# A two-layer transformer kernel: loads of the front in other pieces and order, weight folds at other places, fewer zero products

## What is computed

```python
    def _L0_xattn_ref(modality1, modality2, ln1_g, ln1_b, ln2_g, ln2_b, Wq, bq, Wk, bk, Wv, bv, Wo, bo):
...
        x1 = layernorm(modality1, ln1_g, ln1_b)
        x2 = layernorm(modality2, ln2_g, ln2_b)
        q = x1 @ Wq + bq
        k = x2 @ Wk + bk
        v = x2 @ Wv + bv
        scores = jnp.einsum('bqe,bke->bqk', q, k) * scaling
        attn = jax.nn.softmax(scores, axis=-1)
        ctx = jnp.einsum('bqk,bke->bqe', attn, v)
        return ctx @ Wo + bo
...
            h = jax.nn.gelu(ctx @ w1.T + b1, approximate=False)
            route_logits = (h @ w2.T + b2) / (jnp.abs(tau) + 0.1)
...
            gx = gi @ gru_wih.T + gru_bih
            gh = hs @ gru_whh.T + gru_bhh
...
            slot_values = S_new @ wv.T + bv
            out = jnp.einsum('bts,bsd->btd', alpha, slot_values)
            return out @ wo.T + bo
...
    x = x + _L0_xattn_ref(_layernorm(x, axis=-1), ctx_768, ...)
    x = x + _L0_ffn_ref(_layernorm(x, axis=-1), ...)
    x = x + _L1_xattn_ref(_layernorm(x, axis=-1), ctx_768, ...)
    x = x + _L1_ffn_ref(_layernorm(x, axis=-1), ...)
    return x
```

## Time and profile before

| | |
|---|---|
| median of three runs | 552.25 us (551.52 to 552.89) |
| profiled execution, first to last instruction (span) | 551.06 us |
| profiled execution, time with what lies around the span | not recorded apart; the fastest run is 551.52 us |
| TensorE busy | 538.4 us, 98% |
| VectorE, ScalarE, GpSimd busy | 284.0, 254.1, 168.7 us |
| moved by DMA | 74.30 MB, mean 135 GB/s |

### The profile page before, as it was taken

One profiled execution on the slowest core, in us unless ns is written; L12 is line 12 of the kernel. 1 busy time (PEld: TensorE's weight loads), 2 busy tenths in 40 slices (PEclk: granted clock), 3 DMA queues, 4 the chain that ended last, 5 costly groups with the idle time before them and its releaser, 6 DMA issues.

```text
span 551.1 us, 11061 instructions
## 1 busy us (share of the span) xinstructions
PE 538.4 (98%) x3967; PEld 444.4 (81%) x3968; DVE 284.0 (52%) x847; ACT 254.1 (46%) x587; POOL 168.7 (31%) x152
## 2 busy tenths in 40 slices
PE   9999999999999999999999889999999999999995
PEld 7887878777655676777777679999999999999995
DVE  4867676988562776855788865722212111212110
ACT  1343476263346767687787834542222222222221
POOL 2211000002145222332222043354335454445533
PEclk9999999999999999999999999999999999999999
DMA  8940000000110000300470657968788888898733
GB/s 320 403 141 1 2 0 2 0 1 2 38 39 0 2 2 1 116 1 2 135 287 7 227 172 244 318 187 268 221 246 219 248 229 236 239 255 238 239 66 38
DMA packets 28651, 74.30 MB, mean 135 GB/s; under 512 B 5600, under 2 KB 20320, under 8 KB 23360
## 3 DMA queue, kind: packets, MB, share of 16 engines
q1 hardware_dynamic: 18592, 61.87, 31.9%
q0 software_dynamic: 7488, 10.39, 10.6%
q10 hardware_dynamic: 2528, 1.48, 0.9%
HBM read 62.88 MB, written 10.85 MB: 134 GB/s over the span
## 4 chain that ended last, share of the span: by engine, by line
PE 93%; ACT 4%; DVE 1%; issue 1%; POOL 0%; DVEq 0%; POOLq 0%
PE ps L897 64%; PE ps L1193 12%; PE ps L901 11%; ACT ring L617 2%; PE ps L1041 1%; PE ps L1050 1%; ACT ring L624 1%; PE ps L1053 1%; PE ps L1044 1%; PE ps L981 1%; PE ps L1024 1%; ACT HF L629 0%; ACT ring L658 0%; POOL out_x L422 0%; PE ps L1122 0%
## 5 line engine op out<-in xcount | busy, mean ns | idle before, releaser
L897 PE MATMUL ps<-keep,arena 128*128 128x128 f32 (+2 forms) x976 | 114.9, 274 | 0.0
L897 PEld LDWEIGHTS ps<-keep,arena 128*128 128x128 f32 x976 | 112.8, 192 | 1.5 <-issue 1.1
L2014 DVE TENSOR_TENSOR keep<-keep,ps 128x512 f32<-128x512 f32 x39 | 26.8, 686 | 145.7 <-PE ps L897 124.2
L422 POOL DMA_INDIRECT out_x<-arena,row_no x38 | 59.9, 1576 | 102.1 <-DMA out_x<-arena,row_no 65.2
L1193 PE MATMUL ps<-arena,keep 128*128 x312 | 73.7, 380 | 0.1
L665 ACT COPY keep<-ps 128x256 f32<-128x256 f32 x39 | 14.5, 372 | 107.1 <-PE ps L901 103.8
L381 POOL TENSOR_TENSOR ring<-arena,keep 128x512 f32<-128x512 f32 x32 | 33.5, 1049 | 96.9 <-PE ps L897 79.8
L1193 PEld LDWEIGHTS ps<-arena,keep 128*128 128x128 f32 x312 | 56.4, 190 | 6.6 <-issue 0.3
L617 ACT ACTIVATE ring<-ps,mx 128x128 f32<-128x128 f32 x192 | 52.3, 403 | 6.2 <-DVE mx L1714 6.2
L897 PE MATMUL ps<-ring,arena 128*32 128x128 f32 (+1 forms) x640 | 53.1, 348 | 1.5 <-ACT ring L624 1.4
L373 POOL TENSOR_TENSOR var_x<-var_x,minus_half 128x4 f32<-128x4 f32 x16 | 16.5, 1036 | 115.8 <-DVE var_x L1570 115.8
(11 more groups left out here) (266 smaller groups left out, 816.2 us busy)
## 6 DMA issues: line engine op xcount, KB each, us to landing
arena<-in_w SPq DMA_DIRECT2D x29, 1024.0 KB
w_first<-in_w SPq DMA_DIRECT2D x10, 1024.0 KB
arena<-in_w SPq DMA_DIRECT2D x8, 512.0 KB, 7.3
keep<-in_keep SPq DMA_DIRECT2D x1, 3115.0 KB, 20.8
ring<-in_fold SPq DMA_DIRECT2D x1, 2112.0 KB, 12.7
arena<-in_x SPq DMA_DIRECT2D x4, 512.0 KB, 10.5
arena<-in_ctxT SPq DMA_DIRECT2D x4, 512.0 KB, 7.1
arena<-in_ctx SPq DMA_DIRECT2D x4, 384.0 KB, 11.2
```

Of the source, the lines that this page charges most:

```text
L422: pool.indirect_dma_start(out=out_d, out_offset=bass.IndirectOffsetOnAxis(ap=rows_at, axis=0), in_=YO[t % DEEP], in_offset=None, compute_o ...
L897: ins = pe.matmul(out, w, m, start=(k == 0), stop=(k == len(pairs) - 1))
L2014: dve.tensor_tensor(HA[r % 2], HA[r % 2], ps[:, 2 * (r % 2) + 1, :], ALU.mult).then_inc(act_ok, 1)
```

## The change

The fold weights are packed in another order (whh last), and loaded in four pieces (768, 768, 576 and 768 KB), each with its own semaphore; the rest of `keep` is loaded in two (288 KB of w1 and w2, and the remainder). The first part of `keep` and of the fold weights now stand ahead of the context of group 0. The zero stores move from ScalarE to SyncE, behind the transposed contexts. TensorE has 6 zero products in place of 16 at the start and none in the query bias; fold_value stands directly behind fold_query, and fold_slots ahead of turn_x(1). The bias columns of fold_value go to another bank. ScalarE scales qk and makes two of the four columns of `spread`, ahead of its first copy; VectorE no longer does. On VectorE norm_x(0) stands ahead of norm_c(0), and the folds stand at other places between statistics and norms.

```diff
--- before.py
+++ after.py
@@ -55,12 +55,12 @@
     ("aW1", KD * H1), ("aW2", H1 // P * D), ("gate", KD * 32),
     ("above16", P // 2), ("ones16", P // 2), ("col_no", P), ("before_group", NGRP * NGRP), ("before_expert", NE * NE), ("tile_start", B), ("pick_start", NPICK * B), ("tile_no", NT), ("tile_first", NT), ("expert_no", NE),
 ])
-KEEP_A = KEEP["w1"][0]
+KEEP_A, KEEP_B = KEEP["w1"][0], KEEP["wih"][0]
 FOLD, FOLD_N = columns([
     ("WqT", KD * D), ("WkT", KD * D), ("Wq", KD * D), ("Wo", KD * D), ("WvT", KD * D), ("Wv", KD * D),
-    ("whh", KD * 3 * D), ("fwv", KD * D), ("fwoT", KD * D), ("slots", KD * NSLOT),
+    ("fwv", KD * D), ("fwoT", KD * D), ("slots", KD * NSLOT), ("whh", KD * 3 * D),
 ])
-FOLD_A = FOLD["Wo"][0]
+FOLD_A, FOLD_B, FOLD_C = FOLD["Wo"][0], FOLD["fwv"][0], FOLD["whh"][0]
 ROWS, ROWS_N = columns([
     ("bo", D), ("slot_scale", NSLOT), ("b2", NSLOT), ("tau", 1), ("fbo", D), ("ab2", D),
 ])
@@ -232,7 +232,7 @@
 
 
         keep_in, fold_in, rows_in = sem("keep_in"), sem("fold_in"), sem("rows_in")
-        keep_in2, fold_in2 = sem("keep_in2"), sem("fold_in2")
+        keep_in2, keep_in3, fold_in2, fold_in3, fold_in4 = (sem(t) for t in ("keep_in2", "keep_in3", "fold_in2", "fold_in3", "fold_in4"))
         x_in = [sem(f"x_in{g}") for g in range(NG)]
         c_in = [sem(f"c_in{g}") for g in range(NG)]
         y_in = [sem(f"y_in{g}") for g in range(NG)]
@@ -244,9 +244,9 @@
         names += "".join(f" var_{m} rs_{m}" for m in norms)
         s = {n: sem("s_" + n) for n in names.split()}
         fold_ps, fold_ok = sem("fold_ps"), sem("fold_ok")
-        half_set = sem("half_set")
-
-        blank_set, blank_out, hot_ok, placed = sem("blank_set"), sem("blank_out"), sem("hot_ok"), sem("placed")
+        set_ok = sem("set_ok")
+
+        blank_out, hot_ok, placed = sem("blank_out"), sem("hot_ok"), sem("placed")
         cols_known, cols_far, columns_ok = sem("cols_known"), sem("cols_far"), [sem(f"columns_ok{k}") for k in range(NPICK)]
         counts_read = sem("counts_read")
         pair_ok, pair_ps, pair_known, pair_sum, pair_added = (sem(t) for t in ("pair_ok", "pair_ps", "pair_known", "pair_sum", "pair_added"))
@@ -310,6 +310,8 @@
         def _(sp):
             def rows_of(g):
                 sp.dma_start(X[g], x_g[g]).then_inc(x_in[g], 16)
+
+            def context_rows_of(g):
                 sp.dma_start(CH[g][:, :, 0:DC], c_g[g]).then_inc(c_in[g], 16)
 
             def context_of(g):
@@ -324,17 +326,34 @@
                 if g < EB // GB:
                     sp.dma_start(early_g[g], XH4[g]).then_inc(stored[g], 16)
 
+            def some_keep(lo, hi, landed):
+                sp.dma_start(keep[:, lo:hi], keep_d[:, lo:hi]).then_inc(landed, 16)
+
+            def some_fold(lo, hi, landed):
+                sp.dma_start(ring[:, lo:hi], fold_d[:, lo:hi]).then_inc(landed, 16)
+
             rows_of(0)
-            sp.dma_start(keep[:, 0:KEEP_A], keep_d[:, 0:KEEP_A]).then_inc(keep_in, 16)
-            sp.dma_start(ring[:, 0:FOLD_A], fold_d[:, 0:FOLD_A]).then_inc(fold_in, 16)
+            some_keep(0, KEEP_A, keep_in)
+            some_fold(0, FOLD_A, fold_in)
+            context_rows_of(0)
+            some_fold(FOLD_A, FOLD_B, fold_in2)
             rows_of(1)
-            sp.dma_start(ring[:, FOLD_A:FOLD_N], fold_d[:, FOLD_A:FOLD_N]).then_inc(fold_in2, 16)
+            context_rows_of(1)
+            some_fold(FOLD_B, FOLD_C, fold_in3)
             sp.dma_start(rows[:, :], rows_d.partition_broadcast(P)).then_inc(rows_in, 16)
             rows_of(2)
-            sp.dma_start(keep[:, KEEP_A:KEEP_N], keep_d[:, KEEP_A:KEEP_N]).then_inc(keep_in2, 16)
+            context_rows_of(2)
+            some_keep(KEEP_A, KEEP_B, keep_in2)
+            some_fold(FOLD_C, FOLD_N, fold_in4)
             rows_of(3)
+            context_rows_of(3)
+            some_keep(KEEP_B, KEEP_N, keep_in3)
             for g in range(NG):
                 context_of(g)
+            sp.wait_ge(set_ok, 2)
+            for n in range(2):
+                sp.dma_start(out_d[B * S + n * P:B * S + n * P + P, :], blank[:, 0:D]).then_inc(blank_out, 16)
+            sp.dma_start(xh_d[B * S:B * S + P, :], blank[:, :]).then_inc(blank_out, 16)
             store(0)
             store(1)
             sp.wait_ge(stored[0], 48)
@@ -422,9 +441,9 @@
                 pool.indirect_dma_start(out=out_d, out_offset=bass.IndirectOffsetOnAxis(ap=rows_at, axis=0),
                                         in_=YO[t % DEEP], in_offset=None, compute_op=ALU.add).then_inc(added, 16)
 
-            pool.memset(minus_half[:, :], -0.5).then_inc(half_set, 1)
-            pool.wait_ge(half_set, 1)
-            pool.memset(blank[:, :], 0.0).then_inc(blank_set, 1)
+            pool.memset(minus_half[:, :], -0.5).then_inc(set_ok, 1)
+            pool.wait_ge(set_ok, 1)
+            pool.memset(blank[:, :], 0.0).then_inc(set_ok, 1)
             for g in range(NG):
                 pool.memset(CH[g][:, :, DC:DC + 1], 1.0)
                 pool.memset(CH[g][:, :, DC + 1:D], 0.0).then_inc(s["ch_pad"], 1)
@@ -529,6 +548,15 @@
                 act.wait_ge(s["cT_ps"], g + 1)
                 act.copy(CT[g], ps[:, 2 * g:2 * g + 2, :]).then_inc(s["cT"], 1)
 
+            def spread_slot_bias():
+                for k in range(KD):
+                    act.activation(spread[:, 2 + k, :], ones, ACT.Copy, scale=kept("fbv")[:, k:k + 1])
+
+            def fold_query():
+                act.wait_ge(fold_ps, 1)
+                for m in range(KD):
+                    act.activation(qk[:, m, :], ps[:, 4, m * D:(m + 1) * D], ACT.Copy, scale=kept("ln1_g")[:, m:m + 1])
+
             def query(g):
                 if not g:
                     act.wait_ge(fold_ok, 2)
@@ -681,13 +709,11 @@
                     answer(m, r - 1)
                 gate(m, r + 1)
 
-            act.wait_ge(blank_set, 1)
-            for n in range(2):
-                act.dma_start(out_d[B * S + n * P:B * S + n * P + P, :], blank[:, 0:D]).then_inc(blank_out, 16)
-            act.dma_start(xh_d[B * S:B * S + P, :], blank[:, :]).then_inc(blank_out, 16)
-            act.wait_ge(half_set, 1)
+            act.wait_ge(set_ok, 1)
             act.activation(warm[:, :], minus_half[:, :], ACT.Exp)
             act.wait_ge(keep_in, 16)
+            spread_slot_bias()
+            fold_query()
             rows_turned(0)
             context_turned(0)
             rows_turned(1)
@@ -1225,7 +1251,6 @@
                 ins.then_inc(fold_ps, 1)
 
             def fold_query_bias():
-                idle(4)
                 pe.wait_ge(fold_ok, 1)
                 for m in range(KD):
                     ins = mm(ps[:, 7, m:m + 1], [(WkT[:, k, m * P:(m + 1) * P], u_col[:, k:k + 1]) for k in range(KD)])
@@ -1235,10 +1260,11 @@
                 pe.wait_ge(fold_in2, 16)
                 for m in range(KD):
                     mm(ps[:, 6, m * D:(m + 1) * D], [(WvT[:, k, m * P:(m + 1) * P], Wo[:, k, :]) for k in range(KD)])
-                    ins = mm(ps[:, 5, m:m + 1], [(Wv[:, k, m * P:(m + 1) * P], kept("ln2_b")[:, k:k + 1]) for k in range(KD)])
+                    ins = mm(ps[:, 7, 8 + m:9 + m], [(Wv[:, k, m * P:(m + 1) * P], kept("ln2_b")[:, k:k + 1]) for k in range(KD)])
                 ins.then_inc(fold_ps, 1)
 
             def fold_slots():
+                pe.wait_ge(fold_in3, 16)
                 for m in range(KD):
                     mm(ps[:, 4, m * D:(m + 1) * D], [(fold("fwv")[:, k, m * P:(m + 1) * P], fold("fwoT")[:, k, :]) for k in range(KD)])
                 pe.wait_ge(fold_ok, 3)
@@ -1252,26 +1278,28 @@
 
             def fold_state():
                 pe.wait_ge(fold_ok, 5)
+                pe.wait_ge(fold_in4, 16)
                 for m in range(6):
                     ins = mm(ps[:, 6, m * NSLOT:(m + 1) * NSLOT], [(fold("whh")[:, k, m * P:(m + 1) * P], slots[:, k, :]) for k in range(KD)])
                 ins.then_inc(fold_ps, 1)
 
             def fold_feed_bias():
+                pe.wait_ge(keep_in3, 16)
                 for m in range(H1 // P):
                     ins = mm(ps[:, 7, m:m + 1], [(kept("aW1", KD)[:, k, m * P:(m + 1) * P], kept("abv")[:, k:k + 1]) for k in range(KD)])
                 ins.then_inc(fold_ps, 1)
 
-            pe.wait_ge(blank_set, 1)
-            idle(16)
+            pe.wait_ge(set_ok, 2)
+            idle(6)
             pe.wait_ge(keep_in, 16)
             fold_query()
+            fold_value()
             turn_x(0)
             fold_query_bias()
             turn_context(0)
-            fold_value()
             query(0)
+            fold_slots()
             turn_x(1)
-            fold_slots()
             turn_context(1)
             score(0)
             query(1)
@@ -2030,28 +2058,26 @@
                 dve.wait_ge(keep_in, 16)
                 dve.wait_ge(fold_ps, 1)
                 dve.tensor_tensor(u_col[:, :], ps[:, 5, 0:KD], kept("bq"), ALU.add)
-                for m in range(KD):
```

(13 more changed lines are left out.)

## The result

The changed kernel took 555.63 us (median of 5, 554.35 to 558.31), the kernel before 552.36 us beside it. The ratio is 1.0063, 95% interval 1.0039 to 1.0088: slower by 3.3 us, where 1.8 us less was forecast. On another chip the ratio was 1.0103 (1.0080 to 1.0126). The profiled execution is the slowest of the five (a mean clock of 0.989, the median's is 0.993), 558.31 us, with a span of 556.5 us; its losses are thus larger than the median's. Ratios and their intervals are estimated from the fast executions of a kernel and of the kernel before on the same chip, so they need not be the quotient of two medians.

A forecast was written before the change was run, and what follows sets the result against it. TensorE's nearly gapless queue was taken as the bound: fold_query 3.86 us earlier and 1.63 us of zero products removed, less 3.63 us of new gaps, made 1.86, rounded to 1.8, giving 550.4 us, range 549.2 to 552.9.

The forecast's parts named there:

- fold_query starts at 7.25 instead of 11.11: TensorE's front: the first fold weights land at 7.25 us by bytes ahead, so fold_query starts 3.86 us earlier.
- the late end: First fold weights land at 8.2 us if the stores on the other queue cost the loads nothing.
- 12 passes of 0.428 end at 6.4 us, before the weights at 7.25: TensorE's start: the six zero products left, 12 passes, are done before the fold weights land.
- the sum: TensorE's front: 7.25 + 15.76 + 3.63 puts score(0) at 26.64 us, 1.86 earlier, with rounding 1.8.
- B: Rival: pause puts off TensorE's clock rise through fold_query, costing at most 2.2 us, time 552.6 us; chance 0.14.
- C: Rival: late clock rise slows fold_value too, another 2.62 us, time 555.2 us; chance 0.08.
- Gap (a): TensorE between fold_query's end at 9.89 and fold_value's weights at 10.35: 0.46 us.
- (b): TensorE waits for ScalarE's copy of the turned rows, with only the query bias between: 0.47 us.
- (c): TensorE waits for ScalarE's copy of the turned context, no longer covered by fold_value: 1.32 us.
- Gap (d): TensorE: turn_context(1) stands right behind turn_x(1), without fold_slots between: 1.38 us.
- the shift at score(0): Whatever TensorE's front gains at the first score, 1.8 us forecast, is carried to the kernel's end.
- A: The main forecast, the sum: 1.2 to 2.4 us gained, 549.8 to 551.1 us; chance 0.62.

The follow-up runs named there:

- after_again: The changed kernel unaltered, run and profiled once more on another chip; 556.85 us, ratio 1.0103.
- a_idle10: The changed kernel with 10 zero products at the start in place of 6; 553.26 us, ratio 1.0025.
- b_idle6: The kernel before with 6 zero products at the start in place of 16, nothing else; 554.24 us, ratio 1.0044.
- a_old_idle16_no4: The changed kernel with TensorE's order as before and 16 zero products at the start, but without the four in the query bias; 551.08 us, ratio 0.9990.
- a_pe_old: The changed kernel with all of TensorE's part as before, including 16 and 4 zero products; 552.28 us, ratio 1.0012.
- b_zero_late: The kernel before with the three zero stores moved to SyncE behind the transposed contexts, nothing else; 551.89 us, ratio 0.9998.
- a_old_fold_first: The kernel a_old_idle12 with the first fold weights issued ahead of x of group 0; 549.93 us, ratio 0.9981.
- a_old_idle12: The kernel a_old_idle16_no4 with 12 zero products at the start in place of 16; 552.05 us, ratio 0.9977.
- a_idle16: The changed kernel with 16 zero products at the start in place of 6; 553.69 us, ratio 1.0041.

## Why the prediction was wrong

**"fold_query starts at 7.25 instead of 11.11".** This step failed by 1.8 us. The landing was worked out from bytes ahead at the rate read between two later landings. The weights landed at 9.0. Of the two ends I had given, 6.9 to 7.3 with the stores counted and 8.2 as the late end, neither held it; the context and the second fold weights, forecast the same way, came 1.9 and 1.8 us late too. The rate of the first microseconds is lower than the one I used: 244 GB/s from 1.26 to 6.4 us and 342 to 9.0, where the stretch from 9 us on has 383. And bytes ahead don't set the landing alone. From 0 to 9 us the mean was 238 GB/s, so 9.0 x 238 = 2142 kB had moved by 9.0 us, where 1464 kB (1429.5 KB) reach up to the fold's end. Some 680 kB of loads behind it had thus moved too; the load wasn't done when its place in the queue was reached. Which of the chip's parts held it back is open. The Trainium skill (DMA: Bandwidth & Descriptors, "Issuing engines are not separate DMA queues") says that transfers of all issuing engines interleave. No price of the stores follows from these profiles: taking them away gained 0.5 us in one kernel, and putting them back lost nothing in another, within a spread of 0.8 us.

**"12 passes of 0.428 end at 6.4 us, before the weights at 7.25".** They did, at 6.15, and the sum put the pause behind them at no cost. It became 3.0 us, and the price wasn't the pause but the clock: 2.44 us in fold_query, 0.65 in fold_value, 1.69 in query(0). Rivals B and C had the right place but another mechanism. They had a rise that is put off; the profiles show a clock that had risen, at 0.50 only from the end of the pause on or, in after_again, after 1.1 us of fold_query. C's time, 555.2 against 555.63 us measured, is close by luck: it counts a start 3.86 us earlier (measured 2.03) and 2.62 us for fold_value, and knows nothing of query(0). The chances of the two, 0.14 and 0.08, were too low, since the pause was reckoned from the mis-sized landing as 0.85 us. At its late end, 8.2, it would already have been 1.8 us. The Trainium skill (TensorE: Matmul & The Clock Gate, "What's actually happening") says that activity releases the throttle. These runs agree: mean clock 0.996 to 0.999 with 10 products (a_idle10), 0.988 to 0.994 with 6 (b_idle6).

**The gaps.** Their sum, 3.66 us against 3.63, is right by luck, since two errors cancel. Gap (a), forecast as 0.46, was absent, because the slow fold_query outlasted fold_value's weights (14.16 against 12.1). Gaps (b) and (c) measured 0.46 and 1.35, against 0.47 and 1.32. Gap (d) was 1.48 against 1.38, and 0.37 more stood ahead of score(0), which the sum had missed. ScalarE's written order is the same in both kernels: the copy of turn_x(1), then the scaling of query(0) that score(0) waits for. Before, turn_x(1) stood directly behind query(0), and copy and scaling (25.35 to 27.70) were done beside fold_slots, before 28.50. Now fold_slots stands first, the copy starts at 30.86, and the scaling ends at 33.22. I had not moved ScalarE's own queue past the new order.

**The rest.** Removing the four products, ScalarE's work and the late stores cost and gave what was said (a_old_idle16_no4, a_pe_old, b_zero_late). VectorE's part was mis-timed: it waits for the context, which landed at 10.15 instead of 8.2, so that norm_x(0) ended at 13.3, where it was to be done with u_col near 11.9. That cost nothing in the changed kernel, whose turn_x(0) came at 17.43; in a_pe_old, a_old_fold_first and a_old_idle12 TensorE waited 0.5, 1.2 and 1.5 us for it. That the shift at score(0) reaches the end held within 0.7 us. The upper bound of A's gain was added up too low: landing 6.9 with gaps of 3.2 gives 2.6 us, not 2.4.

**What stays open.** Why the first fold weights land at 8.0 to 9.3 with 662 or 1045.5 KB ahead, with stores beside them or without. Why the first loss of the clock lasted to about 15.6 us in one profile and 20.6 in another. What decides over the second: the changed kernel and a_idle16 were both idle for 1.5 us in the same gaps, and only the first lost the clock there in its profile.

## What to carry to other kernels

Work that only keeps TensorE busy ahead of its first data is sized by when the data land, measured, and not by when they ought to. Before taking such work away, price a landing that doesn't move: the loss here was not the idle time but 7 to 10 us of products behind it at half speed. When steps are reordered on one engine, walk through the helpers' queues too, since a helper's copy that ran beside a later step can come to stand behind it, with all that the helper does next.

## What was not expected of the hardware

The time of the changed kernel is 0.44 us longer for each microsecond at the lower clock, and its executions had between 3 and 16 of these. The clock does not fall with the last product: in the changed kernel's profile it fell 2.7 us after it, and in after_again it was still up when fold_query began, 2.4 us after it, and fell 1.1 us into that work. Its first rise moves too: in 1.26 to 6.40 us the kernels with 16 products had room for 12 to 15 passes, by how early it came. Loads issued ahead of others did not land by their share of bytes: 768 KB landed 4.9 us after issue with nothing ahead, and 6.2 to 7.5 us after issue with 662 KB ahead.
